# Written-out orders, products without a reader, and a first step partly on VectorE in an eight-batch decoder

## The chip, the core and the metric

The kernel runs on one core of one Trainium2 chip. A core has five engines that run side by side, each through its own list of instructions: TensorE (PE, with its weight loads PEld), VectorE (DVE), ScalarE (ACT), GpSimd (POOL) and SyncE (SP), which issues most of the transfers (DMA). They meet at semaphores. The metric is the device time of the whole program in microseconds (us); lower is better.

## The reference

Eight sequences (batches) of 256 tokens with 256 features pass through two decoder layers; everything is float32.

```python
x = x + _L0_attn_ref(_layernorm(x, axis=-1), ...)                # "a": 16 heads
x = x + _L0_xattn_ref(_layernorm(x, axis=-1), ctx_1024, ...)     # "b": mLSTM cell, gates, 4 heads
x = x + _L0_ffn_ref(_layernorm(x, axis=-1), ...)                 # "c": gated MLP + 4096 experts, top 8 of each head
x = x + _L1_attn_ref(_layernorm(x, axis=-1), ...)                # "d": causal attention, one head
x = x + _L1_xattn_ref(_layernorm(x, axis=-1), ctx_1024, mask, ...)   # "e": queries pooled by 16 tokens, masked keys
x = x + _L1_ffn_ref(_layernorm(x, axis=-1), ...)                 # six local-attention layers, each with its MLP
```

In "c" each token picks, by top-k over products with keys, 64 rows (4 heads x 8 experts, a row of a down and of an up embedding) of a table in HBM:

```python
down, up = down_embed[indices], up_embed[indices]
w = jnp.einsum('btd,bthkd->bthk', hidden_states, down)
w = jax.nn.silu(w) * jax.nn.softmax(scores, axis=-1)
experts_states = jnp.einsum('bthk,bthkd->btd', w, up)
```

In each local layer, queries and keys are scaled to unit length by head and rotated (`q * cos * scale + rotate_half(q) * sin * scale`), a token attends to its window of 64 and the one before, and a gated MLP follows.

## The kernel before

**First layers (`first_layers`).** The work on one batch `n` is cut into pieces, such as `a_z` (the scores of layer a), `b_m0`, `c_up3`, `e_y`. A piece has a function on each engine that takes part in it. For each engine `ORDER` lists pieces with an offset; `pieces` walks the steps and adds the offset to the step to get the batch, so that the same list is run through for every step, and at both ends the pieces whose batch does not exist fall out. An engine never leaves this order: if a piece waits, everything behind it on that engine waits too. PSUM banks are handed out in TensorE's order (`PS_COUNT`, six banks).

The experts' rows are fetched by 16 pieces `c_gather0` to `c_gather15` for each batch on GpSimd, four indirect DMAs each (line 405), into a ring of four buffers. VectorE multiplies a buffer with the hidden state (`c_dot`, line 1133), ScalarE takes the tanh (`c_tanh`), VectorE the coefficient (`c_coef`, lines 1145 and 1146), ScalarE writes it on a diagonal (`c_diag`, line 845), TensorE adds the rows (`c_up`, line 629), and only then may the ring's buffer be filled again. Before the first gather of a batch VectorE has to choose its rows: `c_s0` to `c_s3`, `c_pair`, `c_pick0`, `c_pick1` (the last writes `expert`, line 1117).

For batch 0 the pieces up to there form one chain: layer norm of x (`a_stats`, then `a_rstd` on GpSimd, line 392), `a_q`, `a_k`, `a_z` (PE line 487, DVE line 988: scores plus mask), `a_exp`, `a_probs`, `a_o` (497), `a_y` (442), the sum with x (979), then b: `b_hT`, `b_g` (516), `b_scan`, `b_gt` (525), four `b_m` (536 to 539) and four `b_qk` (549, 550), `b_h0`, `b_h1` (558, 567, 568), and on VectorE, ScalarE and GpSimd the division, centring, squares, root and sum (`b_h0`, from line 1036, to `b_add`), then `c_hT` (433), `c_q` (451), `c_s` (589).

SyncE issues in this order: x of batch 0 (`load_x`, line 285), the weights of a, then, behind a wait for two fills of GpSimd (`consts_set`), context 0, the weights of b and part of c, x of batch 1, the other weights, x of batches 2 to 7, and only then what `ORDER["sync"]` lists: `e_ctx`, `b_ctx`, `e_mask` (line 299, read on VectorE by the piece `e_mask`, lines 1189 to 1192). GpSimd writes all constant masks in `start` before its first piece.

**Local layers (`local_layers`).** 48 steps (six layers of eight batches) follow a barrier of all engines. A step's q and k projections are eight pieces of 128 tokens by 512 features; for each, TensorE writes `pj` (line 1657), ScalarE makes `qk_raw` and `qk_sq` of it (1781, 1803), VectorE `ss`, `qk_cos`, `qk_sin` (1924 to 1932), GpSimd the sum of cos and sin part (`qk_rot`, 1598), the norms (1600, 1603) and, for keys, the product with the norm (1608). TensorE turns `qk_rot` (1665). A buffer of `ss`, cos and sin is used by every second piece, so VectorE waits for GpSimd two pieces back. TensorE's first projection of a layer waits for a semaphore (`wqk_loaded`) that counts the q and k weights and the small gain vector of `load_gain` together.

Of the kernel before, what the change touches and what calls it, by code (L numbers as in the profile page):

```python
# [42 lines left out]
def first_layers(nc, xall, x_loaded, ident, ident_bf, shared, dram):  # L43
# [17 lines left out]
    ORDER["tensor"] = [  # L61
# [7 lines left out]
        ("c_up8", -4), ("c_hT", -3), ("e_y", -5), ("e_u", -5), ("c_q1", -3),  # L69
    ]  # L70
    ORDER["scalar"] = [
        ("c_hT", -4), ("c_tanh9", -5), ("c_tanh10", -5), ("c_diag9", -5), ("c_q1", -4), ("c_q0", -4), ("c_diag10", -5), ("a_hT", -2),
        ("c_tanh11", -5), ("b_cT", -3), ("c_diag11", -5), ("c_tanh12", -5), ("b_norm", -3), ("a_q", -2), ("e_k", -5), ("a_k", -2), ("c_diag12", -5),
        ("c_tanh13", -5), ("b_hT", -3), ("a_v", -2), ("c_diag13", -5), ("c_mtanh0", -4), ("c_tanh14", -5), ("c_diag14", -5), ("c_tanh15", -5),
        ("a_exp", -2), ("c_exp", -4), ("c_diag15", -5), ("c_fold", -5), ("c_tanh0", -4), ("c_diag0", -4), ("c_mtanh1", -4), ("d_norm", -5),
        ("c_tanh1", -4), ("d_hT", -5), ("c_diag1", -4), ("b_ln", -3), ("a_o", -2), ("c_tanh2", -4), ("a_norm", -1), ("d_k", -5), ("d_q", -5),
        ("b_low", -3), ("c_diag2", -4), ("d_v", -5), ("c_tanh3", -4), ("d_exp", -5), ("d_pT", -5), ("c_diag3", -4), ("c_tanh4", -4), ("b_m0", -3),
        ("b_m1", -3), ("c_diag4", -4), ("b_m2", -3), ("c_tanh5", -4), ("e_norm", -5), ("b_m3", -3), ("e_v", -5), ("c_tanh6", -4), ("c_diag5", -4),
        ("e_w", -5), ("e_q", -5), ("c_diag6", -4), ("b_sq", -3), ("e_exp", -5), ("c_tanh7", -4), ("c_tanh8", -4), ("e_pT", -5), ("c_diag7", -4),
        ("c_diag8", -4), ("e_cT", -4), ("c_norm", -3), ("e_o", -5), ("e_y", -5),  # L80
    ]
# [2063 lines left out]
```

## Time and profile before

| | |
|---|---|
| device time, median of 3 runs | 3901.14 us (3901.01 to 3903.59) |
| profiled execution: device time | 3898.82 us |
| profiled execution: span of the trace | 3897.1 us |
| first layers, up to the barrier | 0 to 937 us |
| local layers | 937 to 3897 us |
| TensorE busy over the span | 94% |

The span runs from the first instruction to the last. Busy is the share of time in which an engine executes, waits excluded. The granted clock of TensorE is 1.00 at 2.4 GHz and 0.50 at 1.2 GHz. In a row of a timeline, the bracket at the end is how long the engine had been idle before, and what ended it. Products of float32 stand in the trace as two records for each call (a call of `a_z` is four products, its row says x8); a turn (transpose) is one record.

### The profile page before, as it was taken

The page shows a single profiled execution, that of the slowest core. Times are in us where ns is not written, and L with a number is a line of the kernel's source. Part 1 is how long each engine was busy: PE and PEld are TensorE (multiplying, and loading weights), DVE is VectorE, ACT ScalarE, POOL GpSimd, SP SyncE. Part 2 cuts the span into 40 slices and gives each one's busy share as a digit, 9 for nine tenths or more (in the row PEclk, how much of TensorE's full clock was granted, in tenths as well). Part 3 has the DMA queues.
Part 4 walks back from the last instruction along what each step waited for, and adds up shares of the span by engine and source line. Part 5 has one row for each costly group of instructions (what it writes and reads, how often), then busy time and mean ns, then how long its engine had stood idle before and what let it go on. Part 6 is the DMA issues. An engine that isn't in the chain of part 4 may idle for free.

```text
span 3897.1 us, 78634 instructions
## 1 busy us (share of the span) xinstructions
PE 3680.6 (94%) x27016; PEld 2612.3 (67%) x27016; DVE 2758.1 (71%) x9072; ACT 2306.5 (59%) x6802; POOL 2239.6 (57%) x2099
## 2 busy tenths in 40 slices
PE   6899998965799999999999999999999999999997
PEld 4566666643467777777777777677777776777776
DVE  2688888753677777777777777777777777777763
ACT  2355554432566676666666766666667666666663
POOL 1677777763665556556556565565565655655640
PEclk7899999987899999999999999999999999999999
DMA  3777777881000010000000000100100001000000
GB/s 124 159 182 186 184 183 186 180 219 43 1 7 7 4 40 17 28 7 17 28 17 27 7 29 15 33 12 7 40 15 22 14 4 40 15 30 7 4 7 28
DMA packets 111065, 211.64 MB, mean 54 GB/s; under 512 B 22320, under 2 KB 72016, under 8 KB 109136
## 3 DMA queue, kind: packets, MB, share of 16 engines
q0 software_dynamic: 40960, 134.25, 14.3%
q1 hardware_dynamic: 69568, 72.24, 5.8%
q8 instruction: 220, 3.60, 0.4%
q14 instruction: 173, 1.42, 0.1%
q10 hardware_dynamic: 144, 0.13, 0.0%
HBM read 191.92 MB, written 2.10 MB: 50 GB/s over the span
## 4 chain that ended last, share of the span: by engine, by line
PE 70%; issue 2%; DVE 1%; POOL 1%; ACT 1%; DMA 0%; SPq 0%; DVEq 0%; POOLq 0%; ACTq 0%
PE pj L1657 24%; PE pj L1737 12%; PE y_ps L1720 8%; PE y_ps L1746 6%; PE sc L1685 5%; PE tp L1696 5%; PE o_ps L1711 5%; PE tp L1665 4%; PE tp L1635 1%; POOL l_qk_rot L1598 1%; ACT l_probs L1816 0%; DVE l_probs L1953 0%; POOL l_r_k L1603 0%; POOL l_r_q L1603 0%; DVE l_qk_cos L1929 0%
## 5 line engine op out<-in xcount | busy, mean ns | idle before, releaser
L1657 PE MATMUL pj<-w_qkv,l_xT 128*128 128x512 f32 x2304 | 1065.7, 599 | 5.5 <-DMA l_qk_gain<-in_gains 3.3
L1598 POOL TENSOR_TENSOR l_qk_rot<-l_qk_cos,l_qk_sin 128x512 f32<-128x512 f32 x384 | 564.8, 1471 | 842.2 <-DVE l_qk_sin L1932 556.5
L1657 PEld LDWEIGHTS pj<-w_qkv,l_xT 128*128 128x128 f32 x2304 | 414.7, 192 | 385.8 <-issue 376.9
L405 POOL DMA_INDIRECT f_rows<-in_emb,f_expert x512 | 508.3, 993 | 236.3 <-issue 145.8
L1816 ACT ACTIVATE l_probs<-l_probs,l_low 128x128 f32<-128x128 f32 x1536 | 594.1, 391 | 2.1 <-DVE l_low L1953 0.4
L1737 PE MATMUL pj<-l_xnT,l_w 128*128 128x256 f32 x2112 | 511.7, 388 | 2.2 <-issue 1.2
L1924 DVE TENSOR_REDUCE l_ss<-l_qk_sq 128x8 f32<-128x512 f32 x384 | 261.7, 681 | 326.5 <-ACT l_qk_sq L1803 174.9
L1781 ACT ACTIVATE l_qk_raw<-pj 128x512 f32<-128x512 f32 x384 | 227.2, 592 | 435.6 <-PE pj L1657 422.1
L1953 DVE CUSTOM_DVE_ANT_0 l_probs<-sc,l_shut,l_r_q 128x128 f32<-128x128 f32 x1536 | 440.4, 344 | 55.0 <-PE tp L1696 46.7
L1737 PEld LDWEIGHTS pj<-l_xnT,l_w 128*128 128x128 f32 x2112 | 384.5, 191 | 65.2 <-issue 17.4
L1720 PE MATMUL y_ps<-w_o,l_oT 128*128 128x256 f32 x1536 | 341.2, 380 | 3.5 <-ACT l_oT L1781 3.5
L1720 PEld LDWEIGHTS y_ps<-w_o,l_oT 128*128 128x128 f32 x1536 | 292.9, 191 | 63.9 <-issue 22.0
L1603 POOL TENSOR_TENSOR l_r_q<-l_ssm,l_minus_half 128x8 f32<-128x8 f32 x192 | 320.4, 1669 | 16.0
L1603 POOL TENSOR_TENSOR l_r_k<-l_ssm,l_minus_half 128x8 f32<-128x8 f32 x192 | 320.3, 1668 | 16.0
L1929 DVE TENSOR_TENSOR l_qk_cos<-l_qk_raw,l_rope 128x512 f32<-128x512 f32 x384 | 302.5, 788 | 0.0
L1984 DVE TENSOR_SCALAR l_hT<-pj,l_ff_cols 128x256 f32<-128x256 f32 (+1 forms) x282 | 135.3, 481 | 231.5 <-ACT l_gate L1844 231.5
L1816 ACT ACTIVATION_READ_ACCUMULATOR l_probs<-l_probs,l_low 128x1 f32 x1536 | 292.7, 191 | 0.0
L1746 PE MATMUL y_ps<-l_w,l_hT 128*128 128x256 f32 x1128 | 264.5, 385 | 0.5 <-DVE l_hT L1991 0.5
L1696 PEld LDWEIGHTS tp<-identity,l_probs 128*128 128x128 f32 x1536 | 181.0, 142 | 120.3 <-issue 97.1
L1696 PE MATMUL tp<-identity,l_probs 128*128 128x128 f32 x1536 | 240.2, 279 | 15.4 <-DVE l_probs L1963 6.4
L1608 POOL TENSOR_TENSOR l_qk_rot<-l_qk_rot,l_r_k 128x512 f32<-128x512 f32 x192 | 242.5, 1263 | 15.0
L1665 PEld LDWEIGHTS tp<-identity,l_qk_rot 128*128 128x128 f32 x1536 | 188.3, 142 | 89.5 <-issue 68.1
(335 smaller groups left out, 6890.8 us busy)
## 6 DMA issues: line engine op xcount, KB each, us to landing
w_qkv<-in_L_ffn_Wqkv SPq DMA_DIRECT2D x12, 1024.0 KB, 6.9
l_w<-in_ff_w SPq DMA_DIRECT2D x6, 1408.0 KB, 6.0
f_rows<-in_emb,f_expert POOLq DMA_INDIRECT x512
w_o<-in_L_ffn_Wo SPq DMA_DIRECT2D x6, 1024.0 KB, 5.6
...
```

The costliest lines, as they stand in the source:

```text
L405: pool.indirect_dma_start(rows[:, j % RH, k, :], None, dram["emb"], bass.IndirectOffsetOnAxis(ap=expert[:, n % 2, at:at + 1], axis=0)).the ...
L1598: pool.tensor_tensor(qk_rot[:, i % ROTS, :], qk_cos[:, b, :], qk_sin[:, b, :], ALU.add).then_inc(rotated if s == 0 else pool_front, 1)
L1603: pool.tensor_tensor(inv_norm, ssm[:, b, :], minus_half[:, :], ALU.pow).then_inc(pool_front, 1)
L1657: last = pe.matmul(pj[b][:, :], xT[:, k, t * P:(t + 1) * P], w_qkv[:, k, s * INNER + c * 512:s * INNER + (c + 1) * 512], start=(k == 0), s ...
L1665: last = pe.transpose(bank[:, m * P:(m + 1) * P], qk_rot[:, i % ROTS, m * P:(m + 1) * P], ident[:, :])
L1696: last = pe.transpose(bank[:, at:at + P], probs[:, u % 2, 2 * p + x, t * P:(t + 1) * P], ident[:, :])
L1720: last = pe.matmul(y_ps[:, t, :], oT[:, k, t * P:(t + 1) * P], w_o[:, k, :], start=(t == 0 and k == 0), stop=(t == TILES - 1 and k == HP - 1))
L1737: last = pe.matmul(pj[b][:, s * SEQ:(s + 1) * SEQ], w_1[:, k, at:at + P], xnT[:, k, :], start=(k == 0), stop=(k == KC - 1))
L1746: last = pe.matmul(y_ps[:, t, :], hT[:, f, t * P:(t + 1) * P], w_2[:, f, :], start=(f == 0), stop=(f == FC - 1))
L1816: last = nc.scalar.activation(tile, tile, ACT.Exp, bias=low[:, u % 2, at, t:t + 1], scale=-1.0, accum_out=p_sum[:, u % 2, at, t:t + 1])
L1929: nc.vector.tensor_tensor(cos, raw, table(0, 0, DH), ALU.mult)
L1953: last = nc.vector.tensor_tensor_reduce(probs[:, u % 2, at, t * P:(t + 1) * P], sc[x][:, cols], shut[:, t, :], r_q[:, par, t, h:h + 1], 3. ...
```

## The change

1. **Orders.** `ORDER` is no longer a list for one step but, for each engine, the list of every piece with its batch (`a_hT.0 a_q.0 ...`), over all eight batches; `pieces` only reads it. Each engine still has the same pieces, the same number of times. What is different lies mostly in the first batch and the last two, and in single exchanges between.
2. **Products without a reader.** Ahead of 21 pieces of TensorE (`IDLE`) `keep_busy` issues 2 to 97 products of the identity with itself into `acc[0]`, which nobody reads.
3. **Start.** SyncE loads x of batches 1 and 2 earlier. GpSimd writes `head_row` and `unpool` after its first piece (`start_later`), the rest before.
4. **Local layers.** The gain vector has a semaphore of its own, for which only GpSimd waits. In the first step (`n == 0`) VectorE makes the sum `qk_rot` and the keys' product (`first_sum`), GpSimd only the norms (`first_norms`).

```diff
-    def pieces(engine):
-        for step in range(-FIRST, BATCH + LAST):
-            for piece, ahead in ORDER[engine]:
-                if 0 <= step + ahead < BATCH:
-                    yield piece, step + ahead
+    ORDER["vector"] = """
+        a_stats.0 a_shift.0 a_stats.1 e_mask.0 a_shift.1 a_z.0 a_probs.0 a_y.0 b_stats.0 b_shift.0 a_stats.2 a_z.1 a_shift.2 b_g.0 a_probs.1 b_scan.0
...
+    ORDER["sync"] = """
+        e_ctx.0 b_ctx.0 e_mask.0 b_ctx.1 b_ctx.2 b_ctx.3 e_ctx.1 e_mask.1 e_ctx.2 b_ctx.4 e_mask.2 b_ctx.5 e_mask.3 e_ctx.3 e_mask.4 e_ctx.4 b_ctx.6
...
+    IDLE = {"a_q.0": 4, "a_z.0": 4, "a_o.0": 8, "a_o.1": 12, "a_y.1": 13, "b_gt.0": 5, "b_h0.0": 4, "c_hT.0": 97, "c_s0.0": 4, "c_m4.0": 13,
+            "b_gt.1": 14, "d_hT.7": 22, "d_s.7": 9, "d_o.7": 4, "e_hT.7": 18, "e_w.7": 5, "e_q.7": 3, "e_s0.7": 2, "e_pT.7": 35, "e_o.7": 4,
+            "e_u.7": 3}
...
             sp.wait_ge(consts_set, 1)
+            load_x(1)
             b_ctx(0)
...
-            load_x(1)
+            load_x(2)
...
-            for n in range(2, BATCH):
+            for n in range(3, BATCH):
                 load_x(n)
...
+            def start_later(pool):
                 fill(head_row[:, :, :], 1.0)
...
+            def keep_busy(n):
+
+                for _ in range(n):
+                    pe.matmul(acc[0][:, 0, 0:P], ident[:, :], ident[:, :], start=True, stop=True, skip_group_check=True)
+
             for piece, n in pieces("tensor"):
+                keep_busy(IDLE.get(f"{piece}.{n}", 0))
                 do[piece](n)
...
-                             dram["gains"][l, :].rearrange("(a n) -> a n", a=1).broadcast_to([P, 4 * DH])).then_inc(wqk_loaded, 16)
+                             dram["gains"][l, :].rearrange("(a n) -> a n", a=1).broadcast_to([P, 4 * DH])).then_inc(gain_loaded, 16)
...
+            def first_norms(i):
+
+                t, s, c = QK[i]
+                b = i % 2
+                made = sum(2 + QK[x][1] for x in range(i))
+                pool.wait_ge(first_squares, i + 1)
+                pool.tensor_scalar(ssm[:, b, :], ss[:, b, :], 1e-24, None, ALU.max).then_inc(pool_front, 1)
+                pool.wait_ge(pool_front, made + 1)
+                inv_norm = r_q[:, 0, t, 8 * c:8 * c + 8] if s == 0 else r_k[:, b, :]
+                pool.tensor_tensor(inv_norm, ssm[:, b, :], minus_half[:, :], ALU.pow).then_inc(pool_front, 1 + s)
...
-                    pe.wait_ge(wqk_loaded, 48 * (n // BATCH + 1))
+                    pe.wait_ge(wqk_loaded, 32 * (n // BATCH + 1))
...
+            def first_sum(i):
+                t, s, c = QK[i]
+                b = i % 2
+                whole = qk_rot[:, i % ROTS, :]
+                dve.wait_ge(qk_read, i + 1)
+                wait(dve, tp_full, turned(0, "qk_turn", [i - ROTS]) if i >= ROTS else 0)
+                nc.vector.tensor_tensor(whole, qk_cos[:, b, :], qk_sin[:, b, :], ALU.add).then_inc(first_sums if s else rotated, 1)
+                if s == 1:
+                    dve.wait_ge(first_sums, i // 2 + 1)
+                    dve.wait_ge(pool_front, sum(2 + QK[x][1] for x in range(i + 1)))
+                    heads = whole.rearrange("p (h d) -> p h d", h=8)
+                    nc.vector.tensor_tensor(heads, heads, r_k[:, b, :].rearrange("p (h a) -> p h a", a=1).broadcast_to([P, 8, DH]), ALU.mult).then_inc(rotated, 1)
```

VectorE's list near the start of the program, before the change, from the norm of batch 1 to the first layer norm of b (`f_a_p` are the masked scores `a_z`, then the probabilities):

```order
L963 TENSOR_SCALAR f_var_eps_a<-f_mv_a 128x2
L988 SCALAR_TENSOR_TENSOR f_a_p<-fp,f_block_mask 128x256
L990 TENSOR_REDUCE f_a_top<-f_a_p 128x2
L991 TENSOR_SCALAR f_a_neg<-f_a_top 128x2
L971 SCALAR_TENSOR_TENSOR f_shift_a<-f_mv_a,f_rstd_a 128x2
L995 RECIPROCAL f_a_inv<-f_a_sum 128x2
L996 TENSOR_TENSOR f_a_p<-f_a_p,f_a_inv 128x256
L958 BN_STATS f_bn_a<-x_all 128x6 x2
```

The same place now; `f_keep` and `f_shut` are the piece `e_mask.0`:

```order
L1071 TENSOR_SCALAR f_var_eps_a<-f_mv_a 128x2
L1297 TENSOR_SCALAR f_keep<-f_mask_i 128x256
L1299 TENSOR_SCALAR f_shut<-f_keep 128x256
L1300 TENSOR_SCALAR f_keep<-f_keep 128x256
L1079 SCALAR_TENSOR_TENSOR f_shift_a<-f_mv_a,f_rstd_a 128x2
L1096 SCALAR_TENSOR_TENSOR f_a_p<-fp,f_block_mask 128x256
L1098 TENSOR_REDUCE f_a_top<-f_a_p 128x2
L1099 TENSOR_SCALAR f_a_neg<-f_a_top 128x2
L1103 RECIPROCAL f_a_inv<-f_a_sum 128x2
L1104 TENSOR_TENSOR f_a_p<-f_a_p,f_a_inv 128x256
L1087 TENSOR_TENSOR x_all<-fp,x_all 128x512
```

The three instructions of `e_mask.0` have moved ahead of the first scores, and the statistics of batch 2 (which wait for its x) behind the first sum with x.

TensorE's list now, from the last products of `b_h1.0` to the scores of batch 0 (`c_s0`, `c_s1` and so on); `facc<-identity` are the products without a reader:

```order
L669 MATMUL fp<-f_ctx_one,f_b_c 128x65
L670 MATMUL fp<-f_ctx_one,f_b_c 128x65
L888 MATMUL facc<-identity 128x128 x97
L535 MATMUL fp<-identity,f_hc 128x128 x4
L535 MATMUL fp<-identity,f_ctx_b 128x128 x4
L535 MATMUL fp<-identity,f_h_ad 128x128 x4
L553 MATMUL fp<-f_hT_c,f_c_wq 128x256 x8
L888 MATMUL facc<-identity 128x128 x4
L691 MATMUL fp<-f_c_keys,f_c_qT 128x128 x8
L535 MATMUL fp<-identity,f_h_be 128x128 x4
```

Before, `c_hT.0` (the turn of `f_hc`) followed the last row of `b_h1.0` at once; now 97 products stand between them.

## Rows read from the trace of the kernel before

**Rows 1.** The page: granted clock of TensorE in 40 slices of 97 us.
```profile
PEclk7899999987899999999999999999999999999999
```
**Rows 2.** Stretches: length, busy us (count) of PE, PEld, DVE, ACT, POOL, then PEclk.
```profile
52.00:66.00 14.00, 13.22 (x46) 9.12 (x44) 2.45 (x5) 2.93 (x8) 0.00 (x0) 0.50 0.00 1
...
72.00:84.80 12.80, 0.01 (x1) 0.00 (x0) 6.74 (x21) 3.11 (x18) 3.66 (x4) 0.50 0.16 41
...
400.00:500.00 100.00, 95.29 (x748) 68.86 (x750) 83.38 (x365) 52.20 (x175) 73.04 (x75) 0.97 0.73 186
```
**Rows 3.** Timeline of SyncE's queue: start, us, instruction.
```profile
31.34 0.55 SPq L295 DMA_DIRECT2D f_ctx_e<-in_ctx  x1
```
**Rows 4.** Transfers from 30 to 40 us in 40 slices of 0.25 us.
```profile
GB/s 377 393 393 385 389 389 369 393 381 389 381 389 373 381 389 381 385 381 344 348 369 332 352 344 352 336 287 213 156 98 41 0 0 0 0 0 0 0 0 0
```
**Rows 5.** Timeline of VectorE, first batch, and the mask of the last.
```profile
24.18 0.42 DVE L988 SCALAR_TENSOR_TENSOR f_a_p<-fp,f_block_mask 128x256 f32<-128x256 f32 x1 [6.32 <-PE fp L487]
...
33.90 0.75 DVE L958 BATCH_NORM_STATS2 f_bn_a<-x_all 128x6 f32<-128x256 f32 x2 [7.07 <-DMA x_all<-in_x]
...
72.05 0.16 DVE L1036 TENSOR_SCALAR f_b_norm<-fp 128x4 f32<-128x4 f32 x1 [1.99 <-PE fp L568]
...
909.91 0.29 DVE L1189 TENSOR_SCALAR f_keep<-f_mask_i 128x256 f32<-128x256 int32 x1
```
**Rows 6.** Timeline of GpSimd: first root, first gather.
```profile
11.86 0.72 POOL L392 TENSOR_TENSOR f_rstd_a<-f_var_eps_a,f_minus_half 128x2 f32<-128x2 f32 x1 [0.19 <-POOL f_unpool L382]
...
112.50 1.22 POOL L405 DMA_INDIRECT f_rows<-in_emb,f_expert  x1 [27.71 <-DVE f_expert L1117]
```
**Rows 7.** Timeline of TensorE, first batch: start, us, idle before.
```profile
29.72 3.78 PE L442 MATMUL fp<-w_o,f_a_oT 128*128 128x256 f32 x8 [0.69 <-ACT f_a_oT L798]
...
52.39 0.37 PE L525 MATMUL fp<-identity,f_g_in 4*128 4x4 f32 x2
...
66.63 1.97 PE L558 MATMUL fp<-f_ctx_one,f_b_c 128*128 128x65 f32 x8 [1.41 <-DVE f_b_c L1023]
...
84.84 1.11 PE L433 MATMUL fp<-identity,f_hc 128*128 128x128 f32 x4 [12.83 <-ACT f_hc L884]
...
101.97 1.06 PE L487 MATMUL fp<-f_q_ad,f_k_ad 128*128 128x128 f32 x8
102.90 7.14 PE L601 MATMUL fp<-f_hT_c,w_qkv 128*128 128x256 f32 x32
```
**Rows 8.** All gathers of line 405, and two of what their engine waited for.
```profile
L405 POOL DMA_INDIRECT f_rows<-in_emb,f_expert x512: 940/953/1422, 112.5 to 880.1; - x171
...
  PE facc L629: 58.6, 32
...
  DVE f_expert L1117: 31.9, 3
```
**Rows 9.** Timeline of TensorE: the fold of batch 0, and of batch 6.
```profile
221.84 1.08 PE L639 MATMUL fp<-f_e_p,f_pairs 128*64 128x512 f32 x4
...
800.50 1.08 PE L639 MATMUL fp<-f_e_p,f_pairs 128*64 128x512 f32 x4
```
**Rows 10.** Timeline of TensorE: the last batch of the first layers.
```profile
892.83 1.97 PE L639 MATMUL fp<-f_e_p,f_pairs 128*64 128x512 f32 x4 [1.33 <-ACT f_e_p L855]
...
899.03 1.11 PE L433 MATMUL fp<-identity,f_h_ad 128*128 128x128 f32 x4 [4.23 <-ACT f_h_ad L884]
...
927.46 1.12 PE L740 MATMUL fp<-identity,f_e_p 128*128 128x128 f32 x4 [4.65 <-DVE f_e_p L1213]
...
933.69 2.08 PE L769 MATMUL fp<-f_e_y,f_unpool 128*128 128x256 f32 x4 [0.50 <-ACT f_e_y L798]
...
942.64 7.69 PE L1657 MATMUL pj<-w_qkv,l_xT 128*128 128x512 f32 x11 [3.31 <-DMA l_qk_gain<-in_gains]
```
**Rows 11.** Timeline of VectorE: first step of the local layers.
```profile
947.65 0.69 DVE L1924 TENSOR_REDUCE l_ss<-l_qk_sq 128x8 f32<-128x512 f32 x1 [7.72 <-ACT l_qk_sq L1803]
...
958.33 0.69 DVE L1924 TENSOR_REDUCE l_ss<-l_qk_sq 128x8 f32<-128x512 f32 x1 [2.39 <-POOL l_qk_rot L1608]
...
975.12 0.69 DVE L1924 TENSOR_REDUCE l_ss<-l_qk_sq 128x8 f32<-128x512 f32 x1 [2.39 <-POOL l_qk_rot L1608]
...
977.40 0.68 DVE L1865 COPY l_qT<-tp 128x512 f32<-128x512 f32 x1
```

More of the change, by code:

```diff
@@ L60, in first_layers @@
     ORDER = {}
-    ORDER["tensor"] = [
[3 rows of a table removed]
-        ("c_fold", -5), ("c_y0", -4), ("c_up0", -4), ("d_hT", -5), ("a_o", -2), ("d_q", -5), ("c_up1", -4), ("d_k", -5), ("d_v", -5), ("a_y", -2),
[3 rows of a table removed]
[L69 to L81, printed above, removed]
@@ L82, in first_layers @@
-    ORDER["vector"] = [
[4 rows of a table removed]
-        ("c_m7", -4), ("c_dot2", -4), ("a_stats", 0), ("b_scan", -3), ("c_coef2", -4), ("c_dot3", -4), ("d_top", -5), ("e_mask", -5), ("a_y", -2),
-        ("c_coef3", -4), ("c_dot4", -4), ("b_gt", -3), ("d_inv", -5), ("c_coef4", -4), ("d_o", -5), ("b_qk0", -3), ("e_stats", -5), ("c_dot5", -4),
-        ("e_shift", -5), ("b_qk1", -3), ("b_qk2", -3), ("c_coef5", -4), ("b_qk3", -3), ("e_hT", -5), ("c_dot6", -4), ("b_stats", -2), ("c_coef6", -4),
-        ("b_h0", -3), ("b_h1", -3), ("b_centre", -3), ("e_s", -5), ("e_low", -5), ("b_spread", -3), ("c_dot7", -4), ("e_probs", -5), ("c_dot8", -4),
-        ("c_coef7", -4), ("b_add", -3), ("c_coef8", -4), ("c_stats", -3), ("c_shift", -3), ("c_dot9", -4), ("c_dot10", -4), ("c_coef9", -4),
-        ("b_shift", -2), ("c_coef10", -4), ("e_u", -5), ("f_stats", -5), ("c_dot11", -4),
-    ]
@@ new lines, in first_layers @@
+    """.split()
+    ORDER["sync"] = """
+        e_ctx.0 b_ctx.0 e_mask.0 b_ctx.1 b_ctx.2 b_ctx.3 e_ctx.1 e_mask.1 e_ctx.2 b_ctx.4 e_mask.2 b_ctx.5 e_mask.3 e_ctx.3 e_mask.4 e_ctx.4 b_ctx.6
+        b_ctx.7 e_ctx.5 e_mask.5 e_ctx.6 e_mask.6 e_ctx.7 e_mask.7
+    """.split()
+    def pieces(engine):
+        for event in ORDER[engine]:
+            piece, n = event.split(".")
+            yield piece, int(n)
+    IDLE = {"a_q.0": 4, "a_z.0": 4, "a_o.0": 8, "a_o.1": 12, "a_y.1": 13, "b_gt.0": 5, "b_h0.0": 4, "c_hT.0": 97, "c_s0.0": 4, "c_m4.0": 13,
+            "b_gt.1": 14, "d_hT.7": 22, "d_s.7": 9, "d_o.7": 4, "e_hT.7": 18, "e_w.7": 5, "e_q.7": 3, "e_s0.7": 2, "e_pT.7": 35, "e_o.7": 4,
+            "e_u.7": 3}
@@ L354, in start @@
                 pool.sem_inc(consts_set, 1)
+                pool.iota(iota8[:, :], pattern=[[1, TOPK]], base=0, channel_multiplier=0, allow_small_or_imprecise_dtypes=True).then_inc(set_step, 1)
+                made[0] += 1
+                fill(zeros[:, :], 0.0)
+                fill(pooled[:, KC, :], 0.0)
+                fill(e_o[:, 8 * NB:9 * NB], 0.0)
                 fill(block_mask[:, :, :], 0.0)
@@ L362, in start @@
                 select(future[:, :], [[-1, P]], 0, 1, -BIG)
+                fill(pairs[:, :], 0.0)
+                for at in (0, HP):
+                    pool.wait_ge(set_step, made[0])
+                    pool.affine_select(out=pairs[:, :], in_=pairs[:, :], pattern=[[-1, HP]], base=-at, channel_multiplier=1,
+                                       compare_op=ALU.not_equal, fill=1.0).then_inc(set_step, 1)
+                    made[0] += 1
+            def start_later(pool):
                 fill(head_row[:, :, :], 1.0)
@@ L368, in start @@
                 select(unpool[0:QUAD, :], [[-1, SEQ]], BLK - 1, BLK, 0.0)
-                fill(pooled[:, KC, :], 0.0)
-                fill(e_o[:, 8 * NB:9 * NB], 0.0)
-                pool.iota(iota8[:, :], pattern=[[1, TOPK]], base=0, channel_multiplier=0, allow_small_or_imprecise_dtypes=True).then_inc(set_step, 1)
-                made[0] += 1
-                fill(zeros[:, :], 0.0)
-                fill(pairs[:, :], 0.0)
-                for at in (0, HP):
-                    pool.wait_ge(set_step, made[0])
-                    pool.affine_select(out=pairs[:, :], in_=pairs[:, :], pattern=[[-1, HP]], base=-at, channel_multiplier=1,
-                                       compare_op=ALU.not_equal, fill=1.0).then_inc(set_step, 1)
-                    made[0] += 1
                 pool.wait_ge(set_step, made[0])
@@ L420, in _ @@
             start(pool)
-            for piece, n in pieces("gpsimd"):
+            for at, (piece, n) in enumerate(pieces("gpsimd")):
                 do[piece](n)
+                if at == 0:
+                    start_later(pool)
         @block.tensor
@@ L1593, in rotate @@
                 made = n * 20 + sum(2 + QK[x][1] for x in range(i))
+                if n == 0:
+                    first_norms(i)
+                    return
                 pool.wait_ge(qk_read, 8 * n + i + 1)
```

151 lines of the change are left out of this document (140 added, 11 removed), and 13 rows, old and new, of the table ORDER.

## The prediction

> **What bounds the kernel now.** I read the page's clock line first. The reader sees one slice in which TensorE is granted less than nine tenths of its clock, the first [rows 1]. I then cut the run into stretches. Between 400 and 500 us TensorE is busy for 95.29 us of 100, VectorE for 83.38, GpSimd for 73.04; the clock is 0.97. Around 52 to 66 us TensorE works just as densely (13.22 of 14.00) but at 0.50, and from 72 to 84.8 it does nothing at all [rows 2]. So there are three regimes: a start that is a chain through all engines, partly at 1.2 GHz; a middle in which three engines are close to full; and, from 937 us, the local layers, TensorE's.
>
> The grouped lines give the middle its beat: 512 gathers from 112.5 to 880.1 us, 96 us for a batch of 64, and the folds say the same, (800.50 − 221.84)/6 = 96.4 us [rows 8, 9]. GpSimd waits before gathers for two things: 58.6 us in 32 waits for TensorE to free a ring buffer, 31.9 us in 3 waits for the chosen rows, of which the first alone is 27.71 [rows 6, 8]. Everything before 112.5 us thus delays everything behind it; and since the local layers begin after a barrier and need what the drain behind the last gather leaves, a microsecond at either end is a microsecond of the total.
>
> **The start: the mask.** In the order on VectorE `e_mask.0` now stands ahead of `a_shift.1` and `a_z.0`. It reads a transfer. SyncE issues this behind all weights, all x and `e_ctx.0`; that issue began at 31.34 and took 0.55 us [rows 3], so the mask's comes at about 32. The queues still moved about 380 GB/s then, fell to 41 at 37.5 to 37.75, and to nothing [rows 4]. The list in front of the mask is the same set of loads as before (x of batches 1 and 2 only change place). Its 128x256 int32 are 131 KB, 0.34 us at that rate. I put its landing at 38.5. Three operations at 0.29 us and their gaps, as the same piece shows in the last batch [rows 5], end at 39.6, so `a_z.0` begins at about 39.75, where it began at 24.18: **+15.6 us** on batch 0's chain. If the queue served the mask as soon as it is issued, with 2 us to land, `a_z.0` would begin at 35: +11. That is the lower bound; the upper is +17, if the mask shares the tail with context data. What could have hidden it: the piece behind it on VectorE waited 6.32 us for TensorE's scores already [rows 5], and that is inside the difference of start times.
>
> The Trainium skill ("DMA: Bandwidth & Descriptors", section on queues, rings and completion order) has each DMA engine start the descriptors of one queue in order, and so puts the mask behind the loads; the other reading, the mask served at issue, would make the sum 4.7 us smaller.
>
> Other edits at the start: GpSimd writes two fills later, so its first root comes before 11.86 [rows 6], by some 4.5 us; and the statistics of batch 2, which waited 7.07 us for x until 33.90 [rows 5], stand behind the first sum with x. The mask swallows the first. The second, a piece of 0.75 us out of the way, gives −0.6. ScalarE takes one more operation ahead of the first exponential: +0.2.
>
> **The start: the clock.** Products without a reader (4, 4, 8, 12, 13, 5) and the work of batch 1 now fill TensorE's waits before `b_gt.0`. The trace shows full clock where TensorE was dense before; I take it that the clock is at 2.4 GHz from `b_m0.0` on. The 13.22 us there would be 6.6 [rows 2], but `b_m` and `b_qk` alternate with VectorE and ScalarE, so I count −4.7. `b_gt.0`, at 52.39 before [rows 7], gets 12, 13 and 5 calls ahead of it in places where the gaps are shorter: +0.7. `b_h0.0` with 1.97 us for eight records and what follows up to 72 [rows 7] gives −2.6. With these `f_hc` is ready at 84.8 + 15.6 − 0.6 + 0.2 − 4.7 + 0.7 − 2.6 = 93.4.
>
> **The start: 97 products.** They stand between `b_h1.0` and `c_hT.0`, where TensorE waited 12.83 us for `f_hc` [rows 7]. At full clock, 32 records of 256 columns took 7.14 us, 0.223 each, so 0.112 for 128 columns; the row before it says 0.93 us for eight, 0.116 [rows 7]. A call is two records: 97 × 2 × 0.112 = 21.7 us. They outlast the wait by 21.7 − 12.8 = **+8.9 us**, and all of batch 0 is behind them. Behind them `c_hT.0` (1.11 us for four at half clock, [rows 7]) and `c_q.0` run at full clock: −2.8. The first gather would begin at 112.5 + 8.6 + 8.9 − 2.8 = 127.2, less 0.4 for the other products of layer c at full clock: 126.8, **+14.3**. Ends: if a call costs half of what the rows say (only one of the two records carrying columns), 10.9 us, the wait hides them and the front is +5.4; if they all ran at 1.2 GHz, +21 us more.
>
> The Trainium skill ("TensorE: Matmul & The Clock Gate", back-to-back issue gap) gives about 81 ns for a sustained product of 128 columns; by it 194 records last 15.7 us and the sum would be 6.0 us smaller. Rows 7 show 112 to 116 for float32 at full clock, and the measurement decides.
>
> **The middle.** The order of steady state is nearly the old one: single exchanges. Those on VectorE bring the choosing pieces forward by two of the statistics' operations; those on TensorE bring an addition of rows forward in some batches, where the ring makes GpSimd wait. The 58.6 us of ring waits [rows 8] are 7.3 for a batch. But TensorE has only 4.7 us of idle time in 100 and VectorE 16.6 [rows 2], so what the ring gives back, the chain of choosing or TensorE takes. I count −0.8 for each of six batches, **−5**; ends +10 (an exchange that delays the choosing by 1.5 us for each batch) and −20 (a third of the ring waits and a little more).
>
> **Batch 7's gathers.** The orders put pieces of layer c of batch 7 ahead of d and e of batch 6. Of its share of the ring waits, 7.3, I count half: **−4**, ends 0 and −9. The work of batch 6 that is put off must then fit into the drain.
>
> **The drain.** From the fold at 892.83 to the last product of e [rows 10]. `e_y.6` and 22 calls now stand ahead of `d_hT.7`, in a wait of 4.23 us. The engine has idled at half clock by then: 22 × 0.23 = 5.1 us at best, `e_y.6` 2.1 (as 933.69 shows for `e_u`), at the mixed clock about 8: **+3.7**. Before `e_pT.7`, 35 calls, 7.8 us at full clock, stand in 4.65 us: +2.8 to +3.1. Two smaller overshoots (18 calls before `e_hT`, the exchange before `d_pT`): +1.2. Against them, full clock for the products of d and e, of which `e_pT` 1.12 and `e_u` 2.08 are two: −4.5. Sum **+3.3**; ends −5 (all products hidden) and +9 (clock stays at half).
>
> **The boundary and the first local step.** The first projection waited 3.31 us for the gain's transfer [rows 10]; no more. The rotated vectors still need it, so VectorE's first `ss`, at 947.65 after 7.72 us of idle [rows 11], does not gain all of that: −2 to −3. From 958.33 to 975.12, two pairs of pieces took 8.4 us each, each ending in a wait of 2.39 for GpSimd [rows 11]. Now VectorE makes sum and product itself: for a pair of query pieces eight, of key pieces ten operations at 0.69, 5.5 to 6.9 and some semaphores, for a mixed pair 6.6. TensorE's next work hangs on the copy at 977.40 [rows 11], which stands behind the last of these 12 added operations (8.3 us). I put it at 974: **−3.5**, ends −6 and +1 (the added 8.3 us in front of copies that led before). GpSimd's waits were idle time of an engine that isn't full there.
>
> **The sum.** +14.3 − 5 − 4 + 3.3 − 3.5 = +5.1 us against the profiled execution, 3898.8 (span 3897.1 and 1.7 around it), so 3903.9. The median shown is 3901.1, 2.3 above the profiled one: **3906**. What a measurement can tell from no change is 0.2%, 7.8 us: below 3893.3 is faster, above 3908.9 slower.
>
> **Rivals.** *The front is paid in full.* The gathers' beat stays at 96 us since VectorE's choosing of rows and TensorE's 95% bind it, and batch 7 keeps its ring waits: +14.3 + 3.3 − 3.5 = +14.1, 3915. Place: VectorE's wait at `a_z.0` and the 97 calls; price 15.6 + 8.9; it decides as soon as middle and batch 7 together give less than 6.3 us. For it: three engines close to full [rows 2]; against: 7.3 us of ring waits for a batch.
>
> *The products hide.* A call costs half, or what comes before `c_hT.0` is late in the same measure; then the front is +5.4, the drain −1, batch 7 −5, the middle −7: +5.4 − 7 − 5 − 1 − 3.5 = −11.1, 3890. Against it: rows 7; for it: that no row shows this form repeated without weights that change.
>
> *The change does not do what it says.* The clock falls between the products all the same (they fill only 21 waits). Then −4.7, −2.6 and −2.8 go and the 97 last 43 us in place of 21.7 at worst: 3901.1 + 5.1 + 10.1 + 21.7 = 3938. Against it: 0.9 in the second slice, where TensorE was far from dense [rows 1].
>
> *The orders carry.* The mask's price stays, but the ring waits fall by half, 29 us: +14.3 − 29 − 4 + 3.3 − 3.5 = −19, 3882. TensorE's 4.7 us of idle in each 100 hold the middle to about 30, so it is just possible.
>
> **Chances.** The forecast, about even, 0.42. The front in full 0.30; the clock falls 0.04; together slower 0.34. The products hide 0.18, the orders carry 0.06: faster 0.24. The range 3884 to 3922 holds the first three but for the tails; the forecast's own is 3897 to 3912.
>
> **What would show it.** VectorE's first `a_z` at about 39.7, waiting for `f_mask_i` from a transfer; if near 24, the first term falls. `c_hT.0` at about 102 without idle time before it; the first gather at about 127. The distance of folds near 95.6. The drain from `fold.7` to the first projection longer by about 3. Line `ss` first at about 945 on the old scale, without waits for GpSimd. The forecast is wrong if gathers end less than 2 us or more than 12 us later than 880.1.

## The result, and the profile after

The changed kernel takes 3928.78 us (median of 4 runs, 3921.30 to 3929.14), the kernel before 3901.07 (4 runs, 3899.65 to 3903.59) on the same chip. The ratio is 1.0066, with a 95% interval of 1.0054 to 1.0079: slower by about 26 us. The forecast was 3906, "no change", with a range up to 3922. Its span in the profiled execution is 3919.6 us, 22.5 longer than before, and the working below goes by these two profiles. (That execution is the fastest of the four, the median is 7.5 us above it; the one before is 2.3 below its median. So 5 us of the 27.7 between the medians are not in the working.)

The clock line of the page after answers to [rows 1]. The first two slices are better (8 and 9, before 7 and 8). Slices 9 to 11, the end of the first layers and the first local steps, read 8, 8, 8 where 8, 7, 8 stood before. The middle is nines in both, so this line does not show what happened there.

```profile
PEclk8999999988899999999999999999999999999999
```

The start, in the timelines of SyncE, VectorE, TensorE and GpSimd of the changed kernel (start, us, instruction, idle before). They answer to [rows 3], [rows 5], [rows 7] and [rows 6].

```profile
30.94 0.88 SPq L396 DMA_DIRECT2D f_mask_i<-in_mask  x1
```
```profile
37.51 0.29 DVE L1297 TENSOR_SCALAR f_keep<-f_mask_i 128x256 f32<-128x256 int32 x1 [26.93 <-DMA f_mask_i<-in_mask]
...
38.69 0.42 DVE L1096 SCALAR_TENSOR_TENSOR f_a_p<-fp,f_block_mask 128x256 f32<-128x256 f32 x1
```
```profile
78.73 21.88 PE L888 MATMUL facc<-identity 128*128 128x128 f32 x194
100.45 0.60 PE L535 MATMUL fp<-identity,f_hc 128*128 128x128 f32 x4
```
```profile
125.27 1.22 POOL L505 DMA_INDIRECT f_rows<-in_emb,f_expert  x1 [34.92 <-DVE f_expert L1225]
```

VectorE waits 26.93 us for the mask's transfer; the scores follow at 38.69 (24.18 before). The 194 records of the 97 calls take 21.88 us and `c_hT.0` follows without an idle bracket, where it had waited 12.83 us. The first gather starts 12.8 us later.

The folds of batches 0 and 6 in the changed kernel, answering to [rows 9] (four records each: shortest, median and longest in ns, then first and last start in us):

```profile
L741 PE MATMUL fp<-f_e_p,f_pairs x4: 592/618/643, 228.9 to 229.4; 128*64 128x512 f32 x4
```
```profile
L741 PE MATMUL fp<-f_e_p,f_pairs x4: 592/618/643, 828.1 to 828.5; 128*64 128x512 f32 x4
```

The lateness against before is 12.8 us at the first gather, 7.1 at fold 0, 27.6 at fold 6, 24.6 at fold 7 (917.39 against 892.83), 23.3 at the first projection, 22.5 at the end. The last gather starts at 901.0 (880.1 before). So from the first gather on: batch 0 gives back 5.7, **the six batches between folds 0 and 6 lose 20.4**, batch 7's gathers win 3.0, the drain and the boundary 1.2, the rest 0.8.

What TensorE waits for between 230 and 820 us, before and then after (source waited for: us in total, times, longest):

```profile
PE fp L433 <- ACT f_hc L884: 9.2, 6, 2.0
PE facc L629 <- ACT f_diag L845: 6.9, 6, 2.1
```
```profile
PE fp L535 <- ACT f_hc L992: 21.0, 6, 5.5
PE facc L731 <- ACT f_diag L953: 13.4, 10, 4.1
```

and the same stretch as a window, before and after (length, busy us (count) of PE, PEld, DVE, ACT, POOL, then PEclk):

```profile
230.00:820.00 590.00, 542.02 (x4238) 388.05 (x4237) 483.40 (x2136) 295.33 (x994) 425.83 (x431) 0.97 0.75 184
```
```profile
230.00:820.00 590.00, 538.11 (x4140) 381.47 (x4138) 469.88 (x2073) 288.41 (x965) 411.56 (x415) 0.94 0.71 178
```

TensorE is as busy as before, but completes 98 records fewer (2%; a trace can miss a few), as VectorE, ScalarE and GpSimd complete 3 to 4% fewer instructions; its clock is 0.94 in place of 0.97. The waits of `c_hT` (the turn of layer c's normalised state `f_hc`) have more than doubled. One place, batch 6, in TensorE's timeline before and then after. Before, `c_up7.5` and `c_up8.5` (line 629) stood ahead of `c_hT.6`, with 1.05 and 1.59 us of idle time; now only `c_up7.5` does, with 4.70:

```profile
658.18 1.09 PE L629 MATMUL facc<-f_rows,f_diag 64*64 64x256 f32 x16
660.32 1.09 PE L629 MATMUL facc<-f_rows,f_diag 64*64 64x256 f32 x16 [1.05 <-ACT f_diag L845]
663.01 0.66 PE L433 MATMUL fp<-identity,f_hc 128*128 128x128 f32 x4 [1.59 <-ACT f_hc L884]
```
```profile
677.73 1.09 PE L731 MATMUL facc<-f_rows,f_diag 64*64 64x256 f32 x16
683.52 0.80 PE L535 MATMUL fp<-identity,f_hc 128*128 128x128 f32 x4 [4.70 <-ACT f_hc L992]
684.25 1.94 PE L863 MATMUL fp<-f_e_wo,f_e_o 128*32 128x256 f32 x16
...
693.18 1.09 PE L731 MATMUL facc<-f_rows,f_diag 64*64 64x256 f32 x16
```
```profile
695.10 1.02 POOL L505 DMA_INDIRECT f_rows<-in_emb,f_expert  x1 [6.16 <-PE facc L731]
```

`c_up8.5` has moved behind `c_hT.6`. Its place is now a hole of 4.7 us; behind the hole 16 records that took 1.07 at full clock before (at 663.60) take 1.94; `c_up8.5` itself comes at 693.18, 15.5 us behind `c_up7.5`; and GpSimd waits 6.16 us for the buffer that it frees.

### The profile page after: what moved, and what is told of

Read it like the earlier page. It is cut to its first block, busy times and chain, and to the rows that moved or that the text cites. A ratio compares the mean times of both kernels' runs of the same rounds, so it can differ in the third digit from the quotient of the medians.

```text
span 3919.6 us, 79786 instructions
## 1 busy us (share of the span) xinstructions
PE 3733.3 (95%) x27582; PEld 2669.0 (68%) x27582; DVE 2762.8 (70%) x9084; ACT 2307.8 (59%) x6802; POOL 2228.5 (57%) x2087
## 4 chain that ended last, share of the span: by engine, by line
PE 69%; issue 2%; DVE 2%; ACT 1%; POOL 1%; DMA 0%; SPq 0%; DVEq 0%; POOLq 0%; ACTq 0%
PE pj L1780 24%; PE pj L1860 12%; PE y_ps L1843 8%; PE y_ps L1869 6%; PE sc L1808 5%; PE tp L1819 5%; PE o_ps L1834 5%; PE tp L1788 4%; PE tp L1758 1%; POOL l_qk_rot L1721 0%; ACT l_probs L1939 0%; DVE l_probs L2093 0%; DVE l_qk_cos L2054 0%; POOL l_r_q L1726 0%; DMA l_xf<-l_stream 0%
## 5 line engine op out<-in xcount | busy, mean ns | idle before, releaser
L1721 POOL TENSOR_TENSOR l_qk_rot<-l_qk_cos,l_qk_sin 128x512 f32<-128x512 f32 x376 | 554.6, 1475 | 844.3 <-DVE l_qk_sin L2057 559.7
```

Source lines behind the costliest of these rows:

```text
L1721: pool.tensor_tensor(qk_rot[:, i % ROTS, :], qk_cos[:, b, :], qk_sin[:, b, :], ALU.add).then_inc(rotated if s == 0 else pool_front, 1)
```

## The experiments

Ratios are to the kernel before on the same chip, with their 95% interval. For each profile I also give two numbers of the middle (fold 0 to fold 6): its length, and how much of it the low clock took, which is the sum over stretches of 5 us of length times (1 − granted clock). It is not exact: it counts idle stretches at the low clock too.

| kernel | us, median | ratio | first gather | middle | lost to clock | waits of c_hT 2 to 7 |
|---|---|---|---|---|---|---|
| before | 3901.07 | | 112.5 | 578.7 | 20.5 | 9.2 |
| changed | 3928.78 | 1.0066 [1.0054, 1.0079] | 125.3 | 599.1 | 36.0 | 21.0 |
| e1_mid_old | 3903.22 | 1.0005 [0.9994, 1.0017] | 125.7 | 586.9 | 27.2 | 11.2 |
| e2_mid_new | 3916.44 | 1.0039 [1.0024, 1.0054] | 110.9 | 598.1 | 32.4 | 20.9 |
| e3_front | 3914.02 | 1.0041 [1.0027, 1.0054] | 126.1 | 581.4 | 18.7 | 9.2 |
| e4_ends | 3896.75 | 0.9990 [0.9980, 1.0001] | 110.9 | 587.2 | 27.2 | 9.7 |
| e5_after_bold | 3928.66 | 1.0064 [1.0045, 1.0082] | 125.5 | 603.7 | 37.6 | 21.2 |
| e6_before_bnew | 3910.94 | 1.0020 [1.0010, 1.0029] | 113.3 | 587.3 | 25.6 | 7.5 |
| e7_mask_late | 3884.31 | 0.9947 [0.9928, 0.9966] | 103.5 | 583.5 | 23.8 | 8.3 |
| e8_fewer | 3897.99 | 0.9987 [0.9974, 1.0000] | 117.7 | 586.3 | 25.7 | 9.8 |
| e13_after_again | 3934.41 | 1.0060 [1.0044, 1.0077] | 126.2 | 610.3 | 45.9 | 18.5 |
| e14_fill | 3926.41 | 1.0038 [1.0025, 1.0052] | 126.0 | 600.2 | 28.9 | 2.1 |
| e15_8old_again | 3926.30 | 1.0045 [1.0029, 1.0062] | 124.9 | 593.7 | 25.5 | 8.9 |
| e16_both_again | 3885.27 | 0.9935 [0.9919, 0.9952] | 94.8 | 590.3 | 28.9 | 6.2 |

The kernel before took 3899.5 us beside e1 to e4, 3902.5 beside e5 to e8, 3911.4 beside e13 to e16; a difference between runs of different groups is taken from each run's distance to its own kernel before.

The last three columns come from one profile each, and profiles of one kernel scatter: the changed kernel gave 599.1 and 36.0 once, 610.3 and 45.9 (e13) the other time. So they are best read in groups. The seven kernels with the old middle (before, e1, e3, e4, e7, e8, e16) have a mean of 584.9 us with 24.6 lost to the clock, the three with the new one (changed, e2, e13) 602.5 with 38.1. Of the 17.6 us between them 13.5 are the clock's.

Six more runs came from chips on which the kernel before took 4015; they are told at the end.

### Which stretch of the orders costs (e1 to e4)

Each engine's list was cut at two places where both orders have executed the same pieces, on TensorE behind `d_s.1` and behind `e_u.5`, and the parts were combined.

```python
C1 = dict(tensor=192, scalar=181, vector=189, gpsimd=50, sync=9)
C2 = dict(tensor=514, scalar=507, vector=583, gpsimd=161, sync=21)
ORDER[e] = new[e][:C1[e]] + old[e][C1[e]:C2[e]] + new[e][C2[e]:]     # e1_mid_old
ORDER[e] = old[e][:C1[e]] + new[e][C1[e]:C2[e]] + old[e][C2[e]:]     # e2_mid_new: nothing else of the change
ORDER[e] = new[e][:C1[e]] + old[e][C1[e]:]                           # e3_front: with start and IDLE of batches 0, 1
ORDER[e] = old[e][:C2[e]] + new[e][C2[e]:]                           # e4_ends: with IDLE of batch 7, local part
```

e1_mid_old:

> The changed kernel, but in the middle (from the scores of layer d of batch 1 to e_u of batch 5 on TensorE, and the matching stretch on the other engines) every engine follows the old order. Theory M (the single exchanges of the middle cost it): the folds 1 to 6, which fell behind by 17.3 us more, fall behind by under 4, and the time is about 3928.8 - 17 = 3912. Rival P (the old order would do as badly from a start that is shifted, with batches 0 and 1 laid out anew): folds still fall behind by 15 or more, 3925 to 3929.

e2_mid_new:

> The kernel before, and only the middle of the orders (the same stretch) is the new one; start, both ends, the first local step and the products as before. M: slower by the 17 to 20 us that the folds lost, 3918 to 3921. P: within 4 us of 3901.

e3_front:

> The kernel before with the new start only: new orders for batches 0 and 1, the products ahead of pieces of batches 0 and 1, the loads of x and GpSimd's fills as in the change. First gather at about 125 (+12.8). M: fold 0 late by 7 and no more lost later, 3908. P: the folds fall behind further in the old middle, 3920 or more.

e4_ends:

> The kernel before with the new end only: new orders from the routing of batch 7, the products ahead of pieces of batch 7, the first local step partly on VectorE and the gain's own semaphore. Both theories: the changed kernel won 5 us between fold 6 and its end, so 3896; my prediction had -4 + 3.3 - 3.5 for this, 3897.

The new middle alone, in a kernel that has nothing else of the change, costs 16.9 us by the medians and 19.4 between its folds 0 and 6. The old middle behind the new start costs 2.7 (e3) to 8.2 (e1) there. Rival P is out: the shifted start is not what slows the middle. The start alone costs 14.5. The ends give 2.8, near the expected 3896 to 3897, but the interval of e4 holds 1. With the middle the three make 28.6; the change measured 27.7.

That sum closes better than the parts deserve. e1 has the new start and the new ends together, and by e3 and e4 should cost 11.7; it costs 3.7 (3903, theory M said 3912). By e1 the new middle costs the changed kernel 24 us, by e2 16.9. Why start and ends cost less together than apart was not tested.

### Undoing the two terms of the start (e7, e8, e16)

```diff
# e7_mask_late = e1_mid_old with
-    a_stats.0 a_shift.0 a_stats.1 e_mask.0 a_shift.1 a_z.0 ...
+    a_stats.0 a_shift.0 a_stats.1 a_shift.1 a_z.0 ...  e_mask.0 c_s0.0 ...
# e8_fewer = e1_mid_old with
-    "c_hT.0": 97
+    "c_hT.0": 50
# e9_both, e16_both_again: both edits
```

> As e1_mid_old (changed ends, old middle), but VectorE executes e_mask of batch 0 just ahead of c_s0 of batch 0, where it waits for TensorE anyway. Prediction's term: the wait for the mask's transfer was worth 13 to 16 us: a_z of batch 0 at 23 to 24, first gather 13 or so earlier than 125.7, time 3903 - 13 = 3890. Rival: the gathers take it back, as batch 0 did by 4 to 6 of 12.8: 3896.

> As e1_mid_old, but 50 instead of 97 products without a reader ahead of c_hT of batch 0 (11.2 us instead of 21.9; the wait they stand in was 12.8). Prediction's term: the first gather 8 to 9 us earlier, 3903 - 8 = 3895. Rival: the clock falls in the remaining wait and c_q runs at 1.2 GHz, first gather only 5 earlier, 3898.

> e9_both once more: 3879 if the late mask and the fewer products add up, 3884 if not.

TensorE's timeline of e8_fewer, the 50 calls and what follows:

```profile
79.87 11.38 PE L931 MATMUL facc<-identity 128*128 128x128 f32 x100
92.86 0.66 PE L578 MATMUL fp<-identity,f_hc 128*128 128x128 f32 x4 [1.60 <-ACT f_hc L1035]
```

11.38 + 1.60 is about the old wait of 12.8 again, and `c_hT.0` still runs at full clock: 97 calls overran it by 8 to 9 us, as forecast. The first gather gains 8.0. The time gains 8.2, each kernel taken against the kernel before on its own chip (e1 3.7 above, e8 4.5 below). In e7 VectorE's first scores stand in this row, at 18.76 and not at 23 to 24 as expected:

```profile
18.76 0.42 DVE L1139 SCALAR_TENSOR_TENSOR f_a_p<-fp,f_block_mask 128x256 f32<-128x256 f32 x1 [5.20 <-PE fp L632]
```

So the mask's wait costs 19.9 us against the changed kernel without it; 5.4 of that had been the gain of the new start, which the wait hid. The first gather comes 22.2 earlier than in e1, and the time falls by 21.9, taken as for e8 (e7 is 18.2 below its kernel before): what is won at the first gather is won at the end, and the rival that the gathers take it back is not borne out. Both edits together put the first gather at 94.80 and give 0.9935 of the kernel before, 26 us faster, **the lowest ratio of the study**. The intervals of e7 and e16 overlap, and e16's middle is longer in its one profile (590.3 us against 583.5), so that what the fewer products add to the late mask is not settled. On a chip where the kernel before takes 4015 the same kernel (e9) gives 0.9977.

### Where the middle's 20 us come from (e5, e6, e13 to e15)

The first guess was TensorE's stretch of `b_m` and `b_qk`:

```diff
# e5_after_bold: TensorE, batches 2 to 7, batch 6 as example; e6_before_bnew is the reverse in the kernel before
-    b_gt.6 c_up2.5 b_m0.6 d_pT.4 b_qk0.6 c_up3.5 d_o.4 b_m1.6 b_m2.6 b_m3.6 b_qk1.6 b_qk3.6 c_up4.5 e_hT.4 b_qk2.6 e_v.4 b_h0.6
+    b_gt.6 c_up2.5 b_m0.6 d_pT.4 b_qk0.6 b_m1.6 d_o.4 c_up3.5 b_qk1.6 b_m2.6 b_m3.6 b_qk2.6 b_qk3.6 e_v.4 e_hT.4 c_up4.5 b_h0.6
```

> The changed kernel, but on TensorE the stretch from b_gt to b_h0 of batches 2 to 7 is in its old arrangement (b_m and b_qk alternate, then e_v, e_hT, c_up4); all else as in the change. Theory Q (that arrangement costs the middle: VectorE waits in b_qk for a product that now stands behind c_up4 and e_hT, c_coef5 waits behind it, and the clock falls in the run of b_m): most of the middle's 17 us come back, 3910 to 3914, and the waits of c_hT fall from 5 us to 2. Rival R (the cost is spread over all exchanges, those on VectorE too): at most a third comes back, 3922 to 3929.

> The kernel before with only that stretch of TensorE's list in its new arrangement, batches 2 to 7. Q: slower by 12 to 17 us, 3913 to 3917 (against 3901). R: slower by at most 6.

Theory Q does not hold: in the kernel before that arrangement costs 0.2% (8 us, under the 12 to 17 expected), and put back in the changed kernel it gives nothing, and the waits of `c_hT` stay at 21. Then the clock:

```diff
# e14_fill: the changed kernel with, ahead of the wait for f_hc in the turn of layer c
+    FILL = {2: 10, 3: 6, 4: 4, 5: 20, 6: 18, 7: 20}
+    for _ in range(FILL[n]):
+        pe.matmul(here.bank[:, 0:P], ident[:, :], ident[:, :], start=True, stop=True, skip_group_check=True)
# e15_8old_again (= e10_after_8old): the changed kernel, batch 6 as example, the same for batches 5 and 7
# VectorE   e_probs.4 c_dot8.5 c_coef7.5 b_add.6 c_coef8.5 c_stats.6    (was ... c_stats.6 c_dot8.5 c_shift.6 c_dot9.5 c_coef8.5)
# TensorE   c_up7.5 c_up8.5 c_hT.6                                      (was c_up7.5 c_hT.6 ... c_up8.5)
# ScalarE   c_tanh8.5 and c_diag8.5 ahead of c_norm.6                   (c_tanh8.5, c_diag8.5 stood later)
```

> The changed kernel itself, to stand beside the others on the same chip: 1.0066 of the kernel before (1.0054 to 1.0079).

> The changed kernel with more products without a reader: ahead of c_hT of batches 2 to 7 (10, 6, 4, 20, 18, 20 calls, into the bank that c_hT is about to write), just as long as the waits of 1.2 to 5.5 us that the trace shows there. Theory T (between folds 0 and 6 the changed kernel lost 20.4 us, 15.4 of them to TensorE's clock at 1.2 GHz and 5 to waits, and the clock falls in these waits): the share of low clock shrinks, 6 to 12 us come back, ratio 1.0035 to 1.005. Rival U (the clock falls elsewhere all the same, or the late operand is what costs): within 0.001 of the changed kernel.

> e10_after_8old once more, on a chip whose kernel before runs at about 3900 us. S: ratio lower than the changed kernel's by 0.0013 to 0.0023. R: equal to it. What e10 showed on the slow chip (1.0144) would be a third: the old place is worse in the company of the other new orders.

The turn of batches 5 and 7 in the changed kernel and, below, in e14_fill, same chip (TensorE's timeline):

```profile
591.38 1.11 PE L535 MATMUL fp<-identity,f_hc 128*128 128x128 f32 x4 [3.84 <-ACT f_hc L992]
...
795.12 1.11 PE L535 MATMUL fp<-identity,f_hc 128*128 128x128 f32 x4 [5.50 <-ACT f_hc L992]
```
```profile
589.43 0.60 PE L579 MATMUL fp<-identity,f_hc 128*128 128x128 f32 x4
...
788.90 0.66 PE L579 MATMUL fp<-identity,f_hc 128*128 128x128 f32 x4 [1.18 <-ACT f_hc L1041]
```

Behind the wait the turn's four records take 1.11 us, at 1.2 GHz (granted clock 0.50); behind filled waits 0.60 and 0.66. The same holds for all long waits: in the profiles of the changed kernel, e2, e5 and e13, `c_hT` of batches 5 to 7 waits twelve times, 3.84 to 5.92 us, and takes 1.11 to 1.12 eleven times and 0.80 once. Behind shorter waits both lengths occur, 0.66 behind 2.87 us and 1.12 behind 1.23 in the changed kernel.

Useful work is the same in both kernels, and e14 has 78 calls more; still its middle is 10.1 us shorter, and the clock takes 28.9 us in place of 45.9. The middle's difference is no larger than that between the two profiles of the changed kernel; the clock's 28.9 lies below both of them (36.0 and 45.9). The ratio falls from 1.0060 to 1.0038, with intervals that touch, and e14's interval lies below the first measurement's (1.0054 to 1.0079). That is what theory T said.

Putting the real work back (e15) removes the long waits of batches 5 to 7, shortens the middle by 16.6 us in the profile and the loss to the clock to 25.5, which is the old middle's. This profile is of the fastest of its four executions, though, and by the medians e15 gives 8 us (1.0060 to 1.0045, intervals that overlap). So it is shown that the ninth group's exchange makes the long waits and that the clock is lost behind them. For the times, each of the two gives back about 8 us of the 17 (e2) to 24 (e1) that the new middle costs; where the rest goes, rival R's many small exchanges or another cause, is open.

### Runs on chips on which the kernel before takes 4015 us (e9 to e12, e17, e18)

> As e7_mask_late, with 50 in place of 97 products ahead of c_hT of batch 0. The late mask alone gave 3884, the fewer products alone -5 of the time and -8.0 of the first gather. First gather at 95.5 (103.5 - 8.0). If the two add up, 3884 - 5 = 3879; if GpSimd's ring and the later batches take it back, 3884.

> The changed kernel, but the pieces of the ninth group of rows (c_dot8, c_coef8, c_tanh8, c_diag8, c_up8) of batches 4 to 6 stand again ahead of the normalised state of the next batch (c_norm, c_hT) on VectorE, ScalarE and TensorE. Theory S (in the new order c_hT of batches 5 to 7 waits 5 us for its operand with nothing in front of it, the clock falls there, c_up8 comes late and GpSimd waits for its buffer): the waits of c_hT fall to about 2, 5 to 9 us come back, 3920 to 3924. Rival R (cost spread over all exchanges): within 3 us of 3928.8.

> The kernel before with only this move: the ninth group of batches 4 to 6 behind c_norm and c_hT of the next batch. S: c_hT of batches 5 to 7 waits about 5 us, slower by 4 to 8, 3905 to 3909. R: within 3 of 3901.

> The changed kernel with both stretches in the old order: the ninth group of batches 4 to 6, and TensorE's list from b_gt to b_h0 of batches 2 to 7. If the two account for the middle's 17 us (the second alone made before slower by 8, its return alone gave nothing), 3911 to 3914; if each hides the other in part, 3915 to 3920; if other exchanges are behind it, 3925 or more.

> e9_both (new ends, old middle, late mask, 50 products ahead of c_hT of batch 0) and 4 to 10 products without a reader ahead of c_hT of batches 2 to 7, in waits of 1 to 2.9 us. T: the middle of 590 us, 28.9 of it lost to the low clock, gets 2 to 6 us shorter, ratio to the kernel before 0.992 to 0.993 (e16: 0.9935). U: no change, or slower by the products that overrun the shorter waits.

> e12_after_both once more on an ordinary chip: the changed kernel with the ninth group of batches 4 to 6 and TensorE's stretch from b_gt to b_h0 of batches 2 to 7 in their old order. The changed kernel stands at 1.006, with the first of the two put back at 1.0045. If the second adds to it as it cost the kernel before 0.002: 1.0025. If it adds nothing, as it did alone: 1.0045.

Measured: e9 4003.43, ratio 0.9977 [0.9963, 0.9991]; e10 4072.12, 1.0144 [1.0121, 1.0167]; e11 4025.74, 1.0029 [1.0017, 1.0041]; e12 4078.93, 1.0154 [1.0128, 1.0180]; e17 (e9's kernel with 4 to 10 calls ahead of each `c_hT`) 4004.18, 0.9979 [0.9965, 0.9992]; e18 (e12 again) 4076.17, 1.0160 [1.0144, 1.0176]. The changed kernel was not run there, so e10, e12 and e18 can't be set beside it.

e11 says that the ninth group's new place costs the kernel before 0.3% by itself, more than the 4 to 8 us of theory S; its `c_hT` of batches 5 to 7 then wait 4.5 to 6.0 us, as expected. e12 beside e10 says that TensorE's old stretch adds nothing there.

e17 missed its 0.992 to 0.993: with the calls the waits of `c_hT` fall from 15.8 to 3.0 us and the clock takes 52.7 us of the middle in place of 72.8 (profiles of e9 and e17, on two chips), but the ratio stays. That speaks against a gain in time from filling waits of 1 to 3.7 us.

e18 was to tell on an ordinary chip whether the two moved stretches explain the whole middle; it came to such a chip too, so that stays open. The middles of e12 and e18 are 737 and 728 us, that of e9, with the old middle, 691: with both stretches put back and no `c_hT` of batches 2 to 7 waiting over 2.9 us, what is left of the new orders still costs some 40 us there, and no run says where.

All gathers of e11, to be set beside [rows 8]:

```profile
L546 POOL DMA_INDIRECT f_rows<-in_emb,f_expert x512: 940/952/1531, 112.6 to 1006.4; - x171
...
  PE facc L770: 129.8, 46
  remote: 50.8, 30
```

The gathers start at the same time and take as long each, but the last starts 126 us later. Waits that the profile puts down to "remote" appear in the profiles from these chips and in none of the others. Why these chips are so is not settled.

## Why the prediction was wrong

- **The mask, +15.6: right, measured +14.5.** Forecast landing 38.5, measured 37.51, so the mask was not served at its issue (30.94); `a_z.0` forecast at 39.75, measured 38.69. The early scores of the new start, which the sum called swallowed, are worth 5.4 us once the mask is out of the way (e7).
- **The 97 products: right.** Forecast 21.7 us for 194 records, measured 21.88. The rival of hidden products (half price) is out by that row.
- **The clock in the start: right in the sum, not in its premise.** The prediction took 2.4 GHz from `b_m0.0` on. TensorE was busy without a gap there, yet from 70 to 74 us its clock was 0.50:

```profile
70.00:74.00 4.00, 4.00 (x21) 3.12 (x20) 1.10 (x2) 0.86 (x3) 0.00 (x0) 0.50 0.00 2
```

From `b_gt.0` to the last product of `b_h1.0` the work takes 12.9 us in place of 19.6, 6.7 less, where the forecast had 4.7 + 2.6 = 7.3. Part of the 6.7 is that the pieces now follow each other without waits, four `b_m` and then four `b_qk`, and not the clock; how much, no run tells. The first gather was forecast at 126.8 and came at 125.27.
- **The front as time: luck in part.** e3 costs 14.5 us, forecast +14.3. But its first gather is 13.6 late and its fold 0 only 9.0, and its profile is 11.9 longer at the end; the interval is 10.5 to 21 us.
- **Batch 0's gathers** gave 5.7 us back, for which the sum had no term; in e3, where all behind them is old, they give 4.6 back (13.6 late at the first gather, 9.0 at fold 0), and the middle takes 2.7 again.
- **The middle, −5 with ends +10 and −20: this step failed.** It measured +20.4 between the folds, 19.4 with nothing else changed (e2). I had read the single exchanges as harmless since TensorE had 4.7 us of idle in 100, and had priced only the ring's waits and VectorE's chain. What it missed: an exchange on TensorE that takes a piece out of a wait leaves a hole, and behind a hole of 4 to 6 us TensorE worked at half its clock. Of the 20.4 us, 36.0 − 20.5 = 15.5 are the low clock's by these two profiles (13.5 of 17.6 by the means of the groups); what is left are waits and whatever else. I had worked out the clock's price in the start, from the same rows, and the sum has no term for it in the middle, where the view of 400 to 500 us showed 0.97 [rows 2]. I had also misread the clock line [rows 1]: it reads 7, 8 in the first two slices and 8, 7, 8 in slices 9 to 11, not one slice below nine tenths, and the "0.9 in the second slice" that stood against the rival of the falling clock is an 8. Its upper end, +10, allowed an exchange that delays the choosing, not one that costs clock. The sign that it named came: folds 99.9 us apart in place of 95.6, the last gather 20.9 us later and not under 12. How the rest of the middle's cost comes about stays open: filling the waits or putting the ninth group back returns 8 us each of 17 to 24.
- **Batch 7's gathers, −4: measured −3.0.** **The drain, +3.3: measured +1.1** (from fold 7 to the end of the last product of e, 44.0 us in place of 42.9). The 22 calls ahead of `d_hT.7` ran at full clock, 5.18 us for their 44 records, so that the turn starts 7.0 us behind the fold in place of 6.2, where +3.7 was forecast. **The boundary and the first step, −3.5: measured −3.1**, 2.3 of it ahead of the first projection and 0.8 behind. VectorE now makes the sum and the keys' product. It still waits for GpSimd, which the prediction said it would not: 0.90 for the norm in each key piece, where 2.39 stood for the product [rows 11]:

```profile
975.57 0.69 DVE L2067 TENSOR_TENSOR l_qk_rot<-l_qk_cos,l_qk_sin 128x512 f32<-128x512 f32 x1
977.17 0.69 DVE L2072 TENSOR_TENSOR l_qk_rot<-l_qk_rot,l_r_k 128x512 f32<-128x512 f32 x1 [0.90 <-POOL l_r_k L1708]
977.78 0.68 DVE L2047 TENSOR_REDUCE l_ss<-l_qk_sq 128x8 f32<-128x512 f32 x1
```

- The rival "the front is paid in full" (3915) named the side, but its middle was 0. No rival had a middle that loses.
